# Gated expert layer, one core: the work of the first two rounds laid out anew between the engines

## The reference

```
expert_out = jnp.einsum('bnd,edc->bnec', x, expert_w) + expert_b
t = t + jnp.einsum('bnk,bnkc->bnc', top_p, gathered)
```

## Time and profile before

| | |
|---|---|
| runs shown | 1438.19, 1438.88, 1439.15 us (median 1438.88) |
| profiled execution | 1438.13 us, span of its trace 1436.3 us |
| PE, DVE, ACT, POOL busy | 94%, 87%, 73%, 74% of the span |
| round 0, round 1 | 9.7 to 50.2 us, 50.2 to 130.1 us (ACT's first centred group of each, and `parts`) |
| rounds 2 to 10 | 130.1 us to the end |

### The profile page before, as it was taken

The page is one execution under the profiler, slowest core; times in us unless marked ns, Lnnn a source line. Parts: engine busy times, 40 slices in busy tenths (PEclk is TensorE's granted clock), DMA queues, the critical chain, the costliest instruction groups (busy, mean ns, idle before and its releaser), DMA issues.

```text
span 1436.3 us, 33157 instructions
## 1 busy us (share of the span) xinstructions
PE 1345.7 (94%) x11750; PEld 632.1 (44%) x11750; DVE 1247.6 (87%) x1527; ACT 1046.7 (73%) x3949; POOL 1056.1 (74%) x659
## 2 busy tenths in 40 slices
PE   8864999999999999999999999999999998999998
PEld 8853444444444444444444444444444333333332
DVE  6786799978998889988999889998999789987776
ACT  6666888878888788888888788888888434443432
POOL 5334787787778777786777777877877887887765
PEclk9955999999999999999999999999999999999999
DMA  6442466666666666576666566566665565556563
GB/s 225 128 123 65 142 193 196 194 189 203 196 183 213 188 203 202 166 233 185 195 204 206 177 209 193 168 218 194 193 196 158 154 190 165 154 170 190 170 190 116
DMA packets 85877, 259.97 MB, mean 181 GB/s; under 512 B 13776, under 2 KB 13776, under 8 KB 85712
## 3 DMA queue, kind: packets, MB, share of 16 engines
q1 hardware_dynamic: 85712, 257.85, 59.5%
HBM read 206.42 MB, written 51.38 MB: 179 GB/s over the span
## 4 chain that ended last, share of the span: by engine, by line
PE 64%; DVE 16%; issue 8%; POOL 2%; ACT 1%; DVEq 0%; POOLq 0%; ACTq 0%
PE moe L553 37%; PE gb L499 12%; DVE gx L695 10%; PE tm L478 8%; PE tm L492 2%; PE moe L547 2%; PE tm L538 2%; DVE oh L730 2%; PE tm L577 1%; DVE ot L708 1%; DVE u L780 1%; POOL dl L1217 1%; DVE stats L672 1%; ACT gs L982 1%; POOL parts L1173 0%
## 5 line engine op out<-in xcount | busy, mean ns | idle before, releaser
L553 PE MATMUL moe<-gx,wc 128*64 128x448 f32 x3584 | 811.2, 552 | 0.0
L695 DVE TENSOR_TENSOR gx<-gb,xd 128x896 f32<-128x896 f32 x672 | 710.6, 1085 | 96.7 <-PE gb L499 93.0
L1167 POOL TENSOR_TENSOR gx<-gs,xd 128x896 f32<-128x896 f32 x224 | 477.5, 2132 | 279.2 <-ACT gs L982 148.8
L982 ACT ACTIVATE gs<-gb 128x896 f32<-128x896 f32 x224 | 205.4, 917 | 212.1 <-PE gb L499 211.8
L944 ACT ACTIVATE sq<-xct 112x64 f32<-112x64 f32 x1400 | 338.1, 244 | 7.6 <-DVE early_s L682 2.1
L553 PEld LDWEIGHTS moe<-gx,wc 128*64 128x64 f32 x3584 | 217.8, 136 | 230.5 <-issue 198.3
L499 PE MATMUL gb<-s,cg 52*128 52x448 f16 x1792 | 258.6, 356 | 43.9 <-DVE gx L695 37.2
L944 ACT ACTIVATION_READ_ACCUMULATOR sq<-xct 112x1 f32 x1400 | 263.6, 188 | 0.0
L1183 POOL TENSOR_TENSOR tt<-xc,a1s 128x896 f32<-128x896 f32 x112 | 235.9, 2107 | 11.5 <-issue 9.8
L499 PEld LDWEIGHTS gb<-s,cg 52*128 52x128 f16 x1792 | 56.9, 94 | 380.1 <-DVE gx L695 322.4
L478 PEld LDWEIGHTS tm<-rhs,xa 64*112 64x112 f32 x2800 | 171.2, 182 | 32.0 <-issue 17.8
(11 more groups left out here) (94 smaller groups left out, 1102.2 us busy)
## 6 DMA issues: line engine op xcount, KB each, us to landing
xd<-in_x_dram SPq DMA_DIRECT2D x448, 224.0 KB, 4.0
xa<-in_x_dram SPq DMA_DIRECT2D x112, 448.0 KB, 4.4
xc<-in_x_dram SPq DMA_DIRECT2D x112, 448.0 KB, 4.7
out_dram<-ot SPq DMA_DIRECT2D x112, 448.0 KB, 3.5
gx<-in_const_g_dram SPq DMA_DIRECT2D x1, 384.0 KB, 4.6
cf<-in_const_f_dram SPq DMA_DIRECT2D x1, 333.5 KB, 2.8
gx<-in_L_ffn_expert_w_dram SPq DMA_DIRECT2D x1, 128.0 KB, 4.5
cf<-in_L_ffn_expert_b_dram SPq DMA_DIRECT2D x8, 2.0 KB
```

Of the source, the lines that this page charges most:

```text
L553: last = pe.matmul(moe[b * CH:(b + 1) * CH, c, 0:HALF], wc[:, k * CH:(k + 1) * CH], gx[:, u, b, :], start=False, stop=(k == KT - 1), skip_ ...
L695: dve.tensor_tensor(gx[:, i, :, :], gb[:, 2 * slot:2 * slot + 2, 0:HALF], xd[:, v % 2, :, c * HALF:(c + 1) * HALF], ALU.mult).then_inc(sca ...
L982: act.activation(gs[:, j, :, :], gb[:, 2:4, 0:HALF], ACT.Copy).then_inc(gate_out, 1)
L1167: pool.tensor_tensor(gx[:, ND + j, :, :], gs[:, j, :, :], xd[:, v % 2, :, j * HALF:(j + 1) * HALF], ALU.mult).then_inc(scaled_p, 1)
```

## The change

Before the loop: the load of `xa` for step 0 goes out second, `conv_w` is one of the four loads of `ld_first`, the loads of steps 1 to 3 come ahead of the large constants. DVE zeroes a part of `s`, PE multiplies it by itself 8 times (128 x 448, half precision) before it waits for the first loads, and 3 times after its two small setup products. ACT squares one column of ones at once. POOL builds the bands with 5 instructions over 112 x 672 elements before round 0, and moves the other constants' work (5 instructions) to its step 4 of round 1.

Squares of rounds 0 and 1: group 1 of every step goes to POOL, with one multiplication and two additions that fold 64 columns to 32 and then 16, so DVE sums 8 x 16 elements. Group 0 stays with ACT: with one instruction in all steps of round 0 and the odd steps of round 1, with 8 accumulating ones in the even steps of round 1. DVE takes one maximum over the 1024 elements of a step instead of two. ACT's router part comes after both centred groups, and the sigmoid is taken in step 3.

```
             def early_body(r, Bp):                       # DVE
                 for step in range(STEPS):
-                    channel_max(r, step, 0)
-                    if step > 0 and (not Bp or step % 2 == 1):
-                        channel_sum(r, step - 1, 1)
-                    if step == 0 and Bp:
-                        channel_sum(r - 1, STEPS - 1, 1)
+                    if step > 0:
+                        sum_of_pool(r, step - 1)
                     if Bp:
                         gate(r, step, False)
+                    channel_max_of_step(r, step)
+                    if not Bp or step % 2 == 1:
+                        channel_sum(r, step)
...
-                    channel_max(r, step, 1)
-                    channel_sum(r, step, 0)
                     if Bp:
                         gate(r, step, True)
+                sum_of_pool(r, STEPS - 1)

-            def square_group(r, step, g):                # ACT
-                act.wait_ge(centred_out, a_at(r, NGRP, step, g + 1))
+            def square_group(r, step):
+                act.wait_ge(centred_out, a_at(r, NGRP, step, 1))
...
                 if r > 0 or step > 0:
-                    act.wait_ge(summed, summed_at(r, step - 1, g) if step > 0 else summed_at(r - 1, STEPS - 1, g))
+                    act.wait_ge(summed, summed_at(r, step - 1, 0) if step > 0 else summed_at(r - 1, STEPS - 1, 0))

+            def first_body():                            # ACT
+                for step in range(STEPS):
+                    centred_to_sbuf(0, step, 0)
+                    square_group(0, step)
+                    centred_to_sbuf(0, step, 1)
+                    if step == JOIN:
+                        join_early(0)
+
+            def second_body(r):
                 for step in range(STEPS):
                     centred_to_sbuf(r, step, 0)
-                    if Bp and step == 2:
+                    if step == 3:
                         gate_of_conv(r)
+                    if step % 2 == 1:
+                        square_group(r, step)
                     centred_to_sbuf(r, step, 1)
+                    router(r, step)
+                    if step % 2 == 0:
+                        square(r, step, 0)
+                        square(r, step, 1)
...

+            def square_group(r, step):                   # POOL
+                pool.wait_ge(centred_out, a_at(r, NGRP, step, 2))
+                if due(count := a_at(r, NGRP, step - 1, 2)):
+                    pool.wait_ge(summed, summed_at(r, step - 1, 1) if step > 0 else summed_at(r - 1, STEPS - 1, 1))
+                cols = slice(2 * GRP, 4 * GRP)
+                pool.tensor_tensor(sq[:, cols, :], xct[:, step % 2, cols, :], xct[:, step % 2, cols, :], ALU.mult) \
+                    .then_inc(pool_halved, 1)
...
+                pool.tensor_tensor(sq[:, cols, 0:half], sq[:, cols, 0:half], sq[:, cols, half:CH], ALU.add) \
+                    .then_inc(pool_halved, 1)
...
+                pool.tensor_tensor(sq[:, cols, 0:quarter], sq[:, cols, 0:quarter], sq[:, cols, quarter:half], ALU.add) \
+                    .then_inc(pool_squared, 1)

             pool.wait_ge(ld_first, FIRST_LOADS)          # POOL
-            pool.wait_ge(ld_const, LOADS)
...
+            setup_of_band()
+            for step in range(STEPS):
+                square_group(0, step)
...
             def early_body(r):
                 for step in range(STEPS):
                     router(r, step)
+                    square_group(r, step)
                     if step == 1:
                         to_pool(r)
+                    elif step == 4:
+                        setup_of_spreads()

+            def keep_busy(count):                        # PE
+                for _ in range(count):
+                    pe.matmul(tm[:, 0, 0:HALF], s[:, 0, 0:P], s[:, 0, 0:HALF], start=True, stop=True)
+
+            pe.wait_ge(setup_zeros, 1)
+            keep_busy(8)
             pe.wait_ge(ld_first, FIRST_LOADS)
             pe.matmul(gb[:, 1, 0:E], centre, wr[:, :], start=True, stop=True)
             pe.matmul(gb[:, 2, 0:1], centre, mean_col, start=True, stop=True).then_inc(setup_pe, 1)
+            keep_busy(3)
```

More of the change, by code:

```diff
@@ L48 @@
 XA = 7
+EARLY_LOADS = 4
 EARLY = 6
 JOIN = 6
-ACT_STEPS = 7
 QUADS = 4
@@ L293, in squared_at @@
         def squared_at(r, step, n):
[L295 to L299, removed]
+            if r < 2:
+                return (r * STEPS + step) * QUADS // NGRP + min(n, QUADS // NGRP)
+            steps = (min(r, PAIRS) - 2) * STEPS + (step if r < PAIRS else 0)
+            return QUADS * (STEPS + steps) + (n if r < PAIRS else 0)
         def summed_at(r, step, g):
@@ L304, in summed_at @@
                 return NGRP * step + g + 1
-            return NGRP * STEPS + step + (step + 1) // 2 + 1 + (1 - step % 2 if g == 1 else 0)
+            if g == 1:
+                return NGRP * STEPS + step + 1 + (step + 1) // 2
+            odd = step if step % 2 == 1 else step - 1
+            return NGRP * STEPS + odd + (odd + 1) // 2
         def b_done(eng, r, ops, name):
@@ L414, in body @@
                     if A:
-                        begin = (2 if r == 0 else 0) if step == 0 else step + lead
+                        begin = (EARLY_LOADS if r == 0 else 0) if step == 0 else step + lead
                         loads_a(r, pairs[0], range(begin, min(step + lead + 1, STEPS)))
@@ L421, in body @@
                         store(r, pairs, v - 1)
+            sp.dma_start(cf[:, :], const_f).then_inc(ld_first, 16)
             load_a(0, 0)
-            load_a(0, 1)
+            sp.dma_start(cwb[:, :], conv_w.rearrange("o c h w -> o (c h w)").to_broadcast([W, 18])) \
+                .then_inc(ld_first, 16)
+            sp.dma_start(wr[0:CH, :], router_w).then_inc(ld_first, 16)
+            sp.dma_start(wr[CH:P, :], router_w).then_inc(ld_first, 16)
+            for step in range(1, EARLY_LOADS):
+                load_a(0, step)
             for dst, src in (
@@ L906, in _ @@
         def _(act):
+            act.wait_ge(setup_ones, 1)
+            act.activation(sq[:, 0, 0:1], ones[0:W, :], ACT.Square)
             act.wait_ge(setup_dve, 1)
@@ L938, in square @@
                         act.wait_ge(squared, count)
[L939 to L941 removed]
+                    if r < 2:
+                        act.wait_ge(squared, squared_at(r, step, 0))
+                        act.wait_ge(summed, summed_at(r, step - 1, 0) if step > 0 else
+                                    summed_at(r - 1, STEPS - 1, 0))
+                    elif r == 2 and step == 0:
+                        act.wait_ge(summed, summed_at(r - 1, STEPS - 1, quad // 2))
                 to, lo = stats_at(step)
@@ new lines, in setup_of_band @@
+            def setup_of_band():
+                for kw in range(3):
+                    matrix = shift[kw].unsqueeze(1).to_broadcast([W, 6, W])
+                    weight = cwb[:, :].rearrange("p (n k) -> p n k", k=3)[:, :, kw:kw + 1].to_broadcast([W, 6, W])
+                    link(pool.tensor_tensor(band[:, :, :] if kw == 0 else band_part, matrix, weight, ALU.mult))
+                    if kw > 0:
+                        link(pool.tensor_tensor(band[:, :, :], band[:, :, :], band_part, ALU.add))
@@ L1135, in _ @@
             pool.wait_ge(ld_first, FIRST_LOADS)
-            pool.wait_ge(ld_const, LOADS)
             link(pool.tensor_copy(prio[:, :], prio_in))
-            for n in range(6):
-                for kw in range(3):
-                    weight = cwb[:, 3 * n + kw:3 * n + kw + 1].to_broadcast([W, W])
-                    link(pool.tensor_tensor(band[:, n, :] if kw == 0 else band_part, shift[kw], weight, ALU.mult))
-                    if kw > 0:
-                        link(pool.tensor_tensor(band[:, n, :], band[:, n, :], band_part, ALU.add))
@@ L1331, in body @@
                         to_pool(r)
-            for step in range(ACT_STEPS, STEPS):
-                for g in range(NGRP):
-                    square_group(step, g)
             early_body(1)
```

93 lines of the change are left out of this document (48 added, 45 removed).

## The result

| | before | after |
|---|---|---|
| median | 1439.02 us (6 runs) | 1444.36 us (6 runs) |
| lowest to highest | 1438.19 to 1439.74 | 1443.69 to 1444.71 |
| profiled execution, its span | 1438.13, 1436.3 | 1443.69, 1441.9 |

The ratio is 1.0037, 95% interval 1.0026 to 1.0047: 5.3 us slower. Forecast were 1443.9 us, a range from 1432 to 1451, and slower by over 0.2% as the likeliest case.

The account below looks back on a forecast made before the run. Round 0 was taken as bound by PE, then by a new loop of 3.26 us a step, and round 1 by turns between engines, no single one. 1438.13 + 4.8 + 5.6 - 4.6 gave 1443.9 us, range 1432 to 1451.

Parts of the forecast that it names:

- Round 0, +4.8: Start to ACT's start of round 1: late bands and a longer loop cost 4.8 us (bounds +2.5 and +8).
- the loop: Round 0: maximum, sum, ACT's square, centring, next maximum close a loop of 3.26 us a step, against PE's 2.97.
- the late start: Round 0: POOL builds the bands before its first square, free at 13.4; the maximum of step 1 starts at 16.0.
- Up to the sigmoid, +5.6: Round 1 to the sigmoid: 0.6 for POOL, 1.4 to the root, 3.6 behind the convolution (bounds +3 and +7.5).
- The rest of round 1, -4.6: Sigmoid to `parts`: -13.8 removed, collisions 8.9 and moved conversions 0.3 added (bounds -13.6 and 0).
- reductions: DVE, rest of round 1: 2.07 us a step becomes 1.62, saving 5.0 over eleven steps.
- the turn at the widening: Round 1, DVE waiting for centring behind ACT's widening: 4 times 1.63 (6.5) and 2.3 with sigmoid gates go.
- The price of a collision: Round 1: DVE's two-input operations wait for POOL's instruction; 35 at 0.32 make 11.4 us, 2.5 before the sigmoid, 8.9 after.
- the first rival: Collisions in round 1 are cheap: with none, -5.7 and 1432.4 us, faster; under 0.16 each, no longer slower. Chance 0.22.
- Round 2 on, 0: From `parts`, where round 2 begins, the code is the same: nothing counted, the shift passes through.
- The clock: PE at the upper level from the start halves the convolution (4.75 to 2.4): 1441.5 us, no measurable change. Chance 0.18.
- POOL dearer: POOL's strided additions 30% dearer: its round 0 loop passes 3.26, round 1's collisions grow, +4 and +4, 1452. Chance 0.1.

Follow-up runs that it names:

- Experiment 1: Kernel after with DVE's sum of group 0 ahead of the maximum, in round 0 alone: 1439.01 us, ratio 1.000.
- experiment 2: Kernel after with one of the five band operations left (other two taps of the convolution left out): 1441.95 us, ratio 1.0022.
- experiment 6: Kernel after with POOL's squares of step 5 ahead of the router's part and conversions in step 8: 1444.39 us; with the conversions' move alone: 1444.26 us.
- experiment 7: Kernel before with ACT's router part behind both centred groups in round 1, nothing else of the change: 1434.31 us, ratio 0.9969.
- experiment 5: Kernel after with POOL's squares of round 1 cut to one of their eight rows: 1434.54 us, ratio 0.9968.
- experiment 3: Kernel after without its 11 products of zeros: 1444.24 us, ratio 1.0035.
- both ends of 8: Kernel before with early loads, early table load and 8 products of zeros: 1438.87 us; with 11 before the first loads and experiment 7's order: 1430.96 us.
- the first of 6: Kernel after with POOL's squares of step 5 ahead of the router's part and the conversions moved to step 8: 1444.39 us, ratio 1.0042.
- the middle of 8: Kernel before with 8 products of zeros, early loads, early table load and experiment 7's order: 1435.16 us, ratio 0.9972.
- experiment 8: Kernel before with products of zeros, early loads and table load: 1438.87 us; plus experiment 7's order: 1435.16; plus 11 products in place of 8: 1430.96.

## Why the prediction was right

**Round 0, +4.8, measured +4.80.** Each step is in the trace. `ld_first` ended at 5.46 (5.5 taken); the band operations took 1.32 and 1.61 (1.31 and 1.62, interpolated between measured sizes); POOL was free at 13.39 (13.4); the maximum of step 1 came at 15.99 (16.0); then 3.27 a step (3.26). Experiment 1 shows that the loop was the right one, since cutting its link from sum to square brought back everything; experiment 2 shows the late start.

**Up to the sigmoid, +5.6, measured +5.95.** From the start of the round to the root `r` 10.31 us for 8.34, 1.97 more, for 2.0 in the sum; from the convolution's start to the sigmoid 8.77 for 4.79, 3.98 more, for 3.6. The product behind the convolution, the centring and the table load stand there as forecast; the 0.4 is the expert weights, two products of 0.63 us for 0.38 before, so that the centring product began 0.79 behind the convolution's end for 0.36. The centring product itself did not take longer (1.03 for 1.01, 258 ns each). The bounds had put the lower clock there instead. DVE's seven two-input operations took 1.35 more and an operation with one input 0.51 more (below), for 2.5 taken; the forecast counted eight two-input operations, and there are seven.

**The rest of round 1, -4.6, measured -5.63: the total was near and its terms were not.** DVE's sums over this stretch, by instruction:

| DVE from the sigmoid to `parts` | before | after | difference | forecast |
|---|---|---|---|---|
| reductions | 36.6 (49) | 28.0 (34) | -8.6 | -5.0 |
| two-input operations | 18.6 (27) | 25.7 (26) | +7.1 | +8.9 |
| waits for centring | 11.3 | 0 | -11.3 | -8.8 |
| waits for POOL's folds | 0 | 7.0 | +7.0 | not in it |

The four differences make -5.8, for a measured -5.63. The waits removed were larger, and the reductions too: the forecast took eleven steps of 0.45, but before had 41 reductions of stage A in this stretch and after 26, since after had finished step 2's during the longer wait for the sigmoid, while before had some of them still to do. Against that stood the wait for POOL, 7.0, which the forecast had not named as a term. That the sum came out only 1 us off is in part luck. A link between the two errors can be argued, that with DVE quicker POOL's squares and logits are late next, and experiment 6 fits it (the form of that wait does not matter), but no run shows that they must cancel. Nor was the turn at the widening worth its 8.8 by itself: experiment 7 removed it alone and gained 4.4, with 6.5 less of waiting.

The price of a collision, on which the first rival turned (0.32 each, and no slowdown under 0.16), measured 8.5 us more for the two-input operations of the whole round, or about 0.25 each over 34 of them. The rival "collisions are cheap" (1432.4) fell; experiment 5 comes near to what it would have been: with light squares, which also shorten the wait for the folds, the change is faster than before by 0.32%.

**Round 2 on, 0, measured +0.44.** The shift passed through.

**The other rivals.** The clock: the level did rise early, 258 ns a product until 15 us, and then fell under the centring products, as the forecast had argued; without the zeros the time is the same (experiment 3), so this rival gave nothing, in round 0 or in the convolution (4.79). POOL dearer: its strided additions took 0.72 and 0.45 (0.73 and 0.46 taken).

## What to carry to other kernels

When work is shifted between engines in a pipeline with one buffer per stage, write down the closed loop: which instruction waits for which buffer to come free, link by link, each with a duration from a row. The order of two instructions on one engine (maximum before sum) set 3.27 against 2.83 us a step and was worth all of the 5.3 that this change lost. Work that is "free" on POOL is paid by VectorE, in collisions of its two-input operations and in waits for POOL's queue; here both together came to more than the reductions that were saved. Try the parts of such a change one at a time: one reordering alone gave 4.4 us, the whole change cost 5.3.

## What the runs showed of the hardware

**The early clock comes in some executions only, and does not stay.** A kernel with products of zeros has the same instructions each time, but the first rise is on record in some executions and not in others. An execution with it has a mean granted clock of 0.951 to 0.961, the others 0.973 to 0.977 (lower with the rise, for the reason in the next paragraph). It is on record in four of six of after, in four of ten with 8 products on the kernel before, in four of six with 11, and in 34 of 84 over all kernels with such products; in none of the 11 executions of the two kernels without them (experiments 3 and 7), nor in those of before. How long it lasts differs too: in the profiles that have it, the level fell at about 15 us in four (after, experiments 1 and both ends of 8) and before 8 us in three (experiments 2, the first of 6 and the middle of 8). The long kind saved more: round 1 of the kernels of experiment 8 began at 47.07 and 46.26 us in the two profiles that have it and at 49.19 in the one with the short kind, for 50.25 in before. Over the last 30 us of round 0 a PE without a pause, at 0.50, never brought it back. The page "TensorE: Matmul & The Clock Gate" of the Trainium skill, section "Why this matters for your kernels", would have a PE kept busy get the full clock; for these products (64 rows of weights, 74 columns, float32) the windows of experiment 8 disagree. Products between the centred groups of round 0, to hold the level, were not tried.

**The clock column reads 1.00 until the first change is recorded.** In before it stood at 1.00 to 60 us though a product took 391 ns, and in after, where a first rise and fall are on record, the same code reads 0.50 from 15 us on. Only durations tell the level of the first stretch.

**Collisions go both ways and are not for two-input operations alone.** The timeline of after at one of them, POOL and DVE:

```profile
95.98 1.29 DVE L748 TENSOR_TENSOR ge<-lg,top 112x896 bf16<-112x896 f32 x1
96.40 1.46 POOL L1185 TENSOR_TENSOR sq<-sq 112x256 f32<-112x256 f32 x1
...
98.34 2.07 POOL L1259 TENSOR_TENSOR lg<-lg,brb 112x896 f32<-112x896 f32 x1
...
98.62 2.28 DVE L753 TENSOR_TENSOR key<-ge,prio 112x896 bf16<-112x896 bf16 x1
100.38 1.42 POOL L1180 TENSOR_TENSOR sq<-xct 112x512 f32<-112x512 f32 x1
```

POOL's addition of 256, 0.72 alone, began while DVE had the operation of 896 elements and took 1.46. DVE's bfloat16 key, 0.61 at its shortest in this trace, waited for the 2.07 of POOL's addition and took 2.28; then POOL's square, 1.04 alone, took 1.42. The earlier engine finishes first, each time. In round 1 one operation with one input, 224 integers in SBUF (`p`, L806), was stretched as well:

```profile
58.98 0.78 DVE L806 TENSOR_SCALAR p<-e 112x224 int32<-112x224 int32 x1
...
80.18 0.26 DVE L806 TENSOR_SCALAR p<-e 112x224 int32<-112x224 int32 x1
```

The reductions were not: `key_max` took 1.09 in round 1 of all kernels, beside POOL or not.
